# Scoring the tiles of 192 keys with the keys' two parts side by side, in a two-stage attention kernel on one core

## What is computed

```
x = x + 0.5 * ffn(layernorm(x), router_w, router_b, A, Bm)
x = x + attn(layernorm(x), wq_a, q_norm_w, wq_b, wkv_a, kv_norm_w, wkv_b, wo)
x = x + 0.5 * ffn(layernorm(x), router_w, router_b, A, Bm)
```

```
q = rms_norm(x @ wq_a.T) @ wq_b.T            # 128 plain + 64 rope columns a head
kv_c, k_pe = split(x @ wkv_a.T)              # 128 shared latents, 64 shared rope columns
k_nope, v = split(rms_norm(kv_c) @ wkv_b.T)  # 128 + 128 columns a head
scores = (q_nope @ k_nope.T + rope(q_pe) @ rope(k_pe).T) / sqrt(192)
out = softmax(causal(scores)) @ v            # then @ wo.T
```

## Time and profile before

| | us |
|---|---|
| median of 3 runs | 2209.43 (2208.16 to 2210.24) |
| span of the profiled execution | 2207.4 |
| median less that span | 2.0 |
| TensorE busy | 2135.9 (97%) |
| VectorE busy | 1586.2 (72%) |
| ScalarE busy | 1369.9 (62%) |
| GpSimd busy | 1249.0 (57%) |

### The profile page before, as it was taken

One profiled execution on the slowest core, in us unless ns is written; L12 is line 12 of the kernel. 1 busy time (PEld: TensorE's weight loads), 2 busy tenths in 40 slices (PEclk: granted clock), 3 DMA queues, 4 the chain that ended last, 5 costly groups with the idle time before them and its releaser, 6 DMA issues.

```text
span 2207.4 us, 44541 instructions
## 1 busy us (share of the span) xinstructions
PE 2135.9 (97%) x11548; PEld 1807.6 (82%) x11548; DVE 1586.2 (72%) x3415; ACT 1369.9 (62%) x3561; POOL 1249.0 (57%) x1643
## 2 busy tenths in 40 slices
PE   8989999999999999999989989999999999999998
PEld 7967788888888888888778968888888888888877
DVE  7656777777777667777787657777777777777777
ACT  5555666666666666666665556666666666666654
POOL 5335666667666666666554345555555555555543
PEclk9999999999999999999999999999999999999999
DMA  4024444333344444444423143333333333333331
GB/s 161 19 74 135 143 135 143 107 112 102 134 144 139 134 144 142 136 143 142 153 99 131 30 117 114 113 113 113 113 113 113 113 113 113 114 114 113 109 97 77
DMA packets 217104, 258.01 MB, mean 117 GB/s; under 512 B 145616, under 2 KB 174416, under 8 KB 214992
## 3 DMA queue, kind: packets, MB, share of 16 engines
q1 hardware_dynamic: 212432, 244.64, 35.7%
q10 hardware_dynamic: 4608, 12.58, 1.7%
HBM read 127.14 MB, written 79.69 MB: 94 GB/s over the span
## 4 chain that ended last, share of the span: by engine, by line
PE 63%; DMA 13%; POOL 9%; issue 5%; DVE 4%; ACT 3%; SPq 3%; POOLq 1%; ACTq 0%; DVEq 0%
PE ps L865 48%; DMA stage<-in_wo 8%; PE ps L944 5%; PE ps L1246 3%; DMA arena<-arena 2%; PE ps L1190 2%; SPq L760 1%; PE ps L891 1%; POOL arena L2608 1%; PE ps L879 1%; POOL stage L2609 1%; POOL stage L2607 1%; ACT arena L1407 1%; ACT stage L1765 1%; POOL arena L2610 1%
## 5 line engine op out<-in xcount | busy, mean ns | idle before, releaser
L2317 DVE TENSOR_TENSOR xacc<-ps,xacc 128x512 f32<-128x512 f32 x896 | 602.6, 685 | 196.2 <-PE ps L865 182.2
L1949 DVE TENSOR_TENSOR arena<-ps,arena 128x512 fp32r<-128x512 f32 (+4 forms) x744 | 424.9, 576 | 223.4 <-ACT arena L1407 223.3
L865 PE MATMUL ps<-arena,extra 128*128 128x512 f32 x1920 | 523.5, 402 | 5.2 <-DVE xacc L2317 4.9
L1756 ACT ACTIVATE stage<-ps,negmax 128x128 f32<-128x128 f32 (+6 forms) x512 | 260.4, 509 | 333.5 <-DVE negmax L2296 326.9
L865 PE MATMUL ps<-zT,arena 128*128 128x512 f32 (+1 forms) x1746 | 449.3, 402 | 11.5 <-ACT stage L1407 8.7
L1407 ACT ACTIVATE arena<-ps 128x512 fp32r<-128x512 f32 (+4 forms) x744 | 369.7, 507 | 140.7 <-PE ps L865 63.3
L865 PEld LDWEIGHTS ps<-arena,extra 128*128 128x128 f32 x1920 | 342.6, 189 | 88.9 <-DVE xacc L2317 16.1
L865 PEld LDWEIGHTS ps<-zT,arena 128*128 128x128 f32 x1746 | 318.7, 190 | 83.0 <-ACT stage L1407 13.5
L2621 POOL TENSOR_TENSOR extra<-extra_plain,extra 128x256 fp32r<-128x256 f32 (+1 forms) x256 | 223.2, 875 | 192.6 <-ACT extra L1407 191.9
L865 PE MATMUL ps<-arena 128*128 128x512 f32 x960 | 263.1, 409 | 13.7 <-POOL arena L2621 7.5
L1765 ACT ACTIVATE stage<-stage,rrec 128x128 f32<-128x128 f32 (+6 forms) x512 | 238.3, 533 | 52.2 <-DVE rrec L2302 52.2
(11 more groups left out here) (129 smaller groups left out, 3122.6 us busy)
## 6 DMA issues: line engine op xcount, KB each, us to landing
kept_b<-arena SPq DMA_DIRECT2D x16, 3584.0 KB, 11.0
arena<-kept_b SPq DMA_DIRECT2D x112, 512.0 KB, 6.1
arena<-arena SPq DMA_DIRECT2D x128, 128.0 KB, 3.0
stage<-in_wo SPq DMA_DIRECT2D x16, 1024.0 KB, 13.0
stage<-stage SPq DMA_DIRECT2D x248, 64.0 KB, 2.0
extra<-arena SPq DMA_DIRECT2D x120, 128.0 KB, 3.0
kept_q<-arena SPq DMA_DIRECT2D x16, 768.0 KB, 4.1
arena<-kept_q ACTq DMA_DIRECT2D x32, 384.0 KB, 6.1
```

Of the source, the lines that this page charges most:

```text
L865: last = nc.tensor.matmul(dst, w, m, start=start and n == 0, stop=stop and n == len(passes) - 1, skip_group_check=skip)
L1756: nc.scalar.activation(prob[u][:, poff(u, i):poff(u, i) + w], bank_s(i)[:, 0:w], ACT.Exp, bias=negmax[:, k % 2, i:i + 1], accum_out=rowsum ...
L1949: return nc.vector.tensor_tensor(dst, src, part.bitcast(F32), ALU.subtract)
L2317: nc.vector.tensor_tensor(xs, bank_y(k, j), xs, ALU.add).then_inc(y_added, 1)
```

## The change

A tile with up to 192 keys now counts as one with few keys: in even slots tile 2 is scored by three products of 384, 192 and 384 columns in place of five of 192, its two sums lie side by side in 384 of the bank's 512 numbers, ScalarE copies 192 of them, and VectorE adds them. `s_part` takes tile 2's copy in the same 256 columns of `gate_tab` as those of tiles 0 and 1, so the copy waits until tile 1's add is done (the semaphore `summed`). `apart` is called for tiles 0 and 1 where it was before, and for tile 2 at a place of its own in each list of ScalarE: ahead of turned block 2 in every even slot, and in the first bodies ahead of tile 2's exponential. The order on TensorE, VectorE, GpSimd and SyncE is as before.

```diff
     def few_keys(u, i):
 
-        return keys_of(u, i) <= P
+        return keys_of(u, i) <= P + HQ
...
-        s_part = gate_tab[:, 0:2 * P].rearrange("p (a s) -> p a s", a=2)
+        def s_part(i, w):
+
+            return gate_tab[:, (i % 2) * P:(i % 2) * P + w]
...
                 read_fill(p, 0, "q1", PRO[p])
-                apart(p, 0, 0)
+                apart(p, 0, 0, 0, 2)
                 exps(p, 0, 0, 0)
                 exps(p, 0, 0, 1)
                 if p == 0:
                     keep_latents(n)
                     squares(n)
+                    apart(p, 0, 0, 2)
                     exps(p, 0, 0, 2)
...
                     if few_keys(k % 2, i):
                         act.wait_ge(scores_done, 4 * slot_n(p, g, k) + i + 1)
-                        hi(s_part[:, i, 0:w], bank_s(i)[:, w:2 * w]).then_inc(part_out, 1)
+                        if i == 2:
+
+                            act.wait_ge(summed, parts_n(p, g, k, 1))
+                        hi(s_part(i, w), bank_s(i)[:, w:2 * w]).then_inc(part_out, 1)
...
-                    apart(p, g, k)
+                    apart(p, g, k, 0, 2)
                     fills(k, "front")
                     if k == 2 and p == 0:
                         turned(n, before, 0)
...
                         split_a(m, 2)
                         fills(k, "output")
                         split_b(g, T3, last)
+                        apart(p, g, k, 2)
                         turned(n, before, 2)
                         exps(p, g, k, 1)
                         split_b(g, T4, last)
...
                         split_a(m, 1)
                         exps(p, g, k, 1)
                         fills(k, "output")
+                        apart(p, g, k, 2)
                         turned(n, before, 2)
...
                     dve.wait_ge(part_out, parts_n(p, g, k, i))
-                    nc.vector.tensor_tensor(bank_s(i)[:, 0:w], bank_s(i)[:, 0:w], s_part[:, i, 0:w],
+                    nc.vector.tensor_tensor(bank_s(i)[:, 0:w], bank_s(i)[:, 0:w], s_part(i, w),
                                             ALU.add).then_inc(summed, 1)
```

More of the change, by code:

```diff
@@ L1626, in first_body @@
                     exps(p, 0, 2, 0)
-                    apart(p, 0, 2, 1)
+                    apart(p, 0, 2, 1, 2)
                     split_a(unit_n(p, 0, 2), 2)
@@ L1633, in first_body @@
                     split_b(0, T1, first=True)
+                    apart(p, 0, 2, 2)
                     exps(p, 0, 2, 2)
```

## The result

The changed kernel takes **2219.16 us** (2215.61 to 2222.09, 4 runs) where the kernel before, beside it on the same chip, takes 2209.84: a ratio of 1.0049, 95% interval 1.0037 to 1.0062, slower by half a per cent. The forecast was 2220.2, range 2209 to 2228. The profiled execution's span is 2216.7 us, 9.3 more than before, at the same granted clock of 0.995. Of all executions told of here one, of 2984.43 us in the experiment with the copy alone, had a granted clock of 0.654 in place of 0.993 to 0.998, and the ratios leave it out.

What follows compares the result with a forecast made beforehand. TensorE was taken to bound both attention stages, in pair 0 with a loop over the in_wo load that it meets with 0.44 us to spare. 6.6 + 2.4 + 1.8 = +10.8 us on 2209.4 gave 2220.2 us, range 2209 to 2228.

Steps and rivals of the forecast that it cites:

- TensorE's saving, 0.08 us a tile: Tile 2's products: three take 0.462 us instead of 0.54 for five, 5 us over 64 tiles.
- Pair 1, 0.22 us a slot, +6.6: Pair 1's even slots: copy then add delay VectorE's low part and sums, so TensorE's output 3 waits; bounds 3 to 10.5 us.
- Pair 0, 0.16 us a group, +2.4: Pair 0's 15 groups: VectorE's lateness in slot 2, less what the wait at m0 absorbs; bounds 0 to 7 us.
- The slip: Pair 0, slot 2: low part and sum 1 run late, making TensorE 0.68 us later at output 3's load.
- The spare: Pair 0, product m0 at L1190: its 0.44 us wait for the in_wo load would absorb most of 0.60 us.
- The first bodies, +1.8: First body of each pair: slot 1's scores wait for tile 2's exponential, about 0.9 us each; bounds 0 and 2.6.
- VectorE has room: Rival: sums before outputs 2 and 3 may end later, so TensorE keeps its saving, -2.5 us, 2207; chance 0.11.
- pair 0 pays in full: Rival: the DMA loop slips with TensorE, so pair 0 pays 0.60 x 15 = 9 us, 2227; chance 0.16.
- columns alone: Rival: TensorE saves nothing on tile 2; 2209 to 2210 with VectorE's room (chance 0.05), 2221 to 2223 without.
- the change does not take hold: Rival: tile 2 would not get the new form; called small, as 192 keys pass the new limit of 192.
- between 0 and 0.26 us a group: Pair 0: lengthening of the loop over the in_wo load, as ScalarE's copy delays T4's split, GpSimd and SyncE's queue.

Runs made afterwards that it cites:

- the copy alone: Changed kernel without VectorE's add; ScalarE copies 192 columns of a constant table that nobody waits for: 2208.53 us, ratio 1.0009 to the kernel before.
- the products alone: Changed kernel with tile 2's three products but neither ScalarE's copy nor VectorE's add: 2204.88 us beside 2206.96 for the kernel before, ratio 0.9989.
- the longer add: Changed kernel with one more maximum over 128 constants on VectorE behind tile 2's add, both pairs: 2221.58 us, ratio 1.0070 to the kernel before.
- the extra reduction: Kernel before with one more VectorE maximum between turned block 2's low part and sum 0, pair 1's even slots: 2210.68 us, ratio 1.0020.

## Why the prediction was right

The total came within about 1 us (2220.2 against 2219.2), and that closeness is in part luck. The rise was forecast as 10.8 us and measured as 9.3, and the kernel before ran 0.4 us slower beside it (2209.84) than in the runs that I started from (2209.43). Within the rise, 1.8 us too much for pair 0 stand against 0.6 too little for pair 1 and 0.45 too little for the first bodies. The mechanism of the largest term, pair 1's, held as forecast. Term by term:

- **TensorE's saving, 0.08 us a tile.** Right: 0.46 instead of 0.54 us, and 27.24 to 27.16 with the products alone.
- **Pair 1, 0.22 us a slot, +6.6.** Right in mechanism and nearly in size. The copy took 0.32 us (forecast 0.33), and add, mask and maximum held VectorE for 0.94 (1525.10 to 1526.05, forecast 0.94). The low part was 0.26 late (forecast 0.25), the load at 1523.33 (forecast 1523.34), the distance 0.24 longer, so 30 x 0.24 = 7.2 us. Room of 0.02 to 0.03 where I read 0.04 is the difference.
- **Pair 0, 0.16 us a group, +2.4.** Both sides of this small difference were off. The slip: at output 3's load it was 0.67 us (forecast 0.68):

```profile
659.77 0.53 PEld L867 LDWEIGHTS ps<-arena,extra 128*128 128x128 f32 x3 [0.65 <-DVE xacc L2329]
660.57 0.53 PEld L867 LDWEIGHTS ps<-arena,extra 128*128 128x128 f32 x3 [0.27 <-DVE xacc L2329]
```

  The second row begins with output 3's first load. The slot as a whole is 0.60 later in the changed kernel, so it counts as 660.57 - 0.60 = 659.97, against 659.30 before. The low part of B22 then added 0.12, so the distance with slot 2 grew by 0.79 (28.84 to 29.63). The spare: "Of 0.68 - 0.08 = 0.60 the 0.44 of spare time at L1190 takes most" is the step that failed. The other distance shrank by 0.74 (31.90 to 31.16), 0.08 of it in the products, and the rest at m0. I had read the wait in the row of the product, whose idle time counts only from the modelled end of the product ahead. The weight load of the same m0 had waited longer; before and after:

```profile
687.32 0.30 PEld L1190 LDWEIGHTS ps<-stage 128*128 128x128 f32 x2 [0.88 <-DMA stage<-in_wo]
```
```profile
687.96 0.30 PEld L1192 LDWEIGHTS ps<-stage 128*128 128x128 f32 x2 [0.19 <-DMA stage<-in_wo]
```

  0.88 - 0.19 = 0.69 us went, not 0.44, so more of VectorE's slip was covered than forecast. So a group pays 0.79 - 0.74, about 0.04, instead of 0.16: 0.6 us over pair 0's loop instead of 2.4.
- **The first bodies, +1.8.** Somewhat low. The scores of slot 1 now wait 1.70 us in both (start, as in the earlier trace rows, of the two pairs):

```profile
130.96 0.71 PE L867 MATMUL ps<-keyT,arena 128*128 128x320 f32 x3 [1.70 <-ACT stage L1765]
...
1274.79 0.71 PE L867 MATMUL ps<-keyT,arena 128*128 128x320 f32 x3 [1.70 <-ACT stage L1765]
```

  In pair 1 that is 0.82 more than before (0.88), in pair 0 1.43 more (0.27, which I had not read). Together 2.25.

The sum by these measured terms is 7.2 + 0.6 + 2.25 = 10.0 us, beside 9.3 more in the two spans and in the two medians. What lies between: the stages ahead of the first and behind the last attention, which the change does not touch, were 1.8 and 0.8 us shorter in the profiled execution of the changed kernel, and some 1.8 us more than these terms went in the groups next to the first bodies and on the way into pair 1. About 1.0 of the latter is one wait, of the product at 1373.94 for GpSimd's low part, 1.26 us against 0.28 in the kernel before. It varies from kernel to kernel in these traces, 1.0 with the products alone and none with the change in pair 1 alone or with the longer add, so I don't count it as a cost of the change. The rest I have not traced.

Of the rivals, *VectorE has room* is refuted by the extra reduction, *pair 0 pays in full* by its 0.04 a group, *columns alone* by the products alone, and *the change does not take hold* by the tile's three products in the trace. The bound "between 0 and 0.26 us a group" for the loop over the DMA was right to be there: the copy alone lengthens that loop by 0.26. It did not show in the changed kernel, because TensorE was later than the load anyway.

## What to carry to other kernels

An engine that is idle a quarter of the time can still be without room at one place: look for the load that starts just behind the sum it waits for, and take the distance between the two, not the engine's share, as the price limit. When a change saves time on the bounding engine by giving a helper a step in series (copy, then add), weigh the saving (0.08 us a tile) against the lateness of whatever stands behind that step in the helper's order (0.26 us); the order can be cut so that only the urgent part is ahead. And read spare time at a wait from the weight load's row as well as from the product's.

## What the runs showed of the hardware

VectorE's low part, whose two inputs both lie in SBUF here, and GpSimd's operations on SBUF did not run at once. The later one ended a fixed time behind the first, as if it had stood still until then: about 0.55 us (VectorE, 128x512) or 1.16 us (GpSimd). VectorE's 0.69 became 1.57, 1.32 and 0.88 us by how long GpSimd still had to run, and GpSimd's 1.30 became 1.59. VectorE's sums with one input in PSUM were not held, 0.69 us beside GpSimd. The Trainium skill (SBUF — State Buffer, SBUF: two separate sides) has it so, an exclusive lock that a VectorE operation with two SBUF inputs takes against a GpSimd operation that reads SBUF, and these rows agree. A change that shifts VectorE by 0.6 us can thus turn round who waits for whom.

A wait costs TensorE some 0.1 us more than the idle time shown ahead of the product. The two products of m0 start 0.53 us apart in the kernel before, behind idle times of 0.33 to 0.44, and 0.43 to 0.49 apart in the changed kernel. It isn't peculiar to a DMA: behind the load at 1528.17, which waited for a sum, the product starts at 1528.18 and the next at 1528.51, 0.33 later, while products of 512 columns without a wait start 0.23 apart.
